# Post-norm decoder layer on one core: value projection cut into four parts, a second bank for three projections, max rows sent ahead of stacks

## What is computed

```python
x = layernorm(x + attn(x))          # 16 heads of 32, causal, q k v o projections with bias
x = layernorm(x + wkv(x, ctx))      # keys = x, values = ctx, a recurrence over 256 tokens in log space
x = layernorm(x + ffn(x))           # gate = softmax(x @ W_gate.T), top 1 of 16 heads picks k and v of a token;
                                    # causal attention of 16 query heads against that one k, v
```

## Time and profile before

| | |
|---|---|
| median of 3 runs | 1622.03 us |
| the profiled execution | 1626.53 us, its span 1624.7 us |
| TensorE matmuls | 1423.6 us busy, 88% |
| VectorE | 1103.8 us, 68% |
| ScalarE | 644.2 us, 40% |
| GpSimd | 415.5 us, 26% |
| mean granted TensorE clock | 0.976 of full speed |

### The profile page before, as it was taken

One profiled execution on the slowest core, in us unless ns is written; L12 is line 12 of the kernel. 1 busy time (PEld: TensorE's weight loads), 2 busy tenths in 40 slices (PEclk: granted clock), 3 DMA queues, 4 the chain that ended last, 5 costly groups with the idle time before them and its releaser, 6 DMA issues.

```text
span 1624.7 us, 28990 instructions
## 1 busy us (share of the span) xinstructions
PE 1423.6 (88%) x9792; PEld 1129.7 (70%) x9792; DVE 1103.8 (68%) x2260; ACT 644.2 (40%) x1459; POOL 415.5 (26%) x550
## 2 busy tenths in 40 slices
PE   6879988898998989889899998989989898999866
PEld 5667777766777767777677777777777767777554
DVE  4375766858577676776758667685766858577665
ACT  3442533434344243533435344253433425353322
POOL 1251321414122140321314122141312414122130
PEclk9889999999999999999999999999999999999979
DMA  5432231333213232231333312233221333323111
GB/s 173 140 85 66 58 78 45 84 86 77 73 44 84 68 87 79 58 79 52 78 85 76 78 48 74 70 86 86 67 73 46 74 86 76 89 55 81 37 33 34
DMA packets 63214, 119.70 MB, mean 74 GB/s; under 512 B 14304, under 2 KB 32736, under 8 KB 63072
## 3 DMA queue, kind: packets, MB, share of 16 engines
q1 hardware_dynamic: 60400, 112.56, 27.6%
q10 hardware_dynamic: 2672, 5.24, 0.9%
HBM read 32.81 MB, written 8.39 MB: 25 GB/s over the span
## 4 chain that ended last, share of the span: by engine, by line
PE 54%; DVE 21%; ACT 7%; issue 7%; SPq 6%; DMA 4%; POOL 1%; DVEq 0%; ACTq 0%; POOLq 0%
PE pp L482 9%; PE pp L484 8%; PE pp L483 8%; PE po L580 5%; SPq L320 5%; DVE neg_max L1349 5%; DVE w_key L1426 4%; DMA q_stack<-max_rows 3%; PE po L584 2%; PE sq L528 2%; PE sq L522 2%; PE sk L507 2%; PE sq L507 2%; PE po L594 2%; PE sk L558 2%
## 5 line engine op out<-in xcount | busy, mean ns | idle before, releaser
L1010 ACT ACTIVATE prob<-sk 128x512 f32<-128x512 f32 x384 | 215.0, 594 | 433.2 <-PE sk L507 432.6
L1349 DVE TENSOR_REDUCE neg_max<-sq 128x2 f32<-128x512 f32 (+1 forms) x384 | 249.5, 676 | 54.1 <-PE sq L507 29.5
L482 PE MATMUL pp<-xt_hi,w_hi 128*128 128x256 f32 x728 | 220.6, 303 | 9.7 <-DVE w_lo L1336 7.1
L483 PE MATMUL pp<-xt_lo,w_hi 128*128 128x256 f32 x728 | 207.7, 285 | 0.0
L484 PE MATMUL pp<-xt_hi,w_lo 128*128 128x256 f32 x728 | 207.7, 285 | 0.0
L482 PE MATMUL pp<-w_hi,xt_hi 128*128 128x512 f32 x372 | 159.6, 429 | 27.5 <-DVE q_lo L1464 15.8
L482 PEld LDWEIGHTS pp<-xt_hi,w_hi 128*128 128x128 f32 x728 | 141.2, 194 | 17.4 <-issue 11.9
L483 PE MATMUL pp<-w_lo,xt_hi 128*128 128x512 f32 x372 | 148.5, 399 | 0.0
L484 PE MATMUL pp<-w_hi,xt_lo 128*128 128x512 f32 x372 | 148.4, 399 | 0.0
L1021 ACT ACTIVATE o_ch<-po 128x512 f32<-128x512 f32 x128 | 76.2, 595 | 181.8 <-PE po L584 181.8
L483 PEld LDWEIGHTS pp<-xt_lo,w_hi 128*128 128x128 f32 x728 | 141.4, 194 | 0.7
(11 more groups left out here) (216 smaller groups left out, 3372.2 us busy)
## 6 DMA issues: line engine op xcount, KB each, us to landing
q_stack<-q_hi SPq DMA_DIRECT2D x256, 128.0 KB, 2.3
q_stack<-q_lo SPq DMA_DIRECT2D x128, 128.0 KB, 2.4
k_stack<-k_hi SPq DMA_DIRECT2D x128, 128.0 KB, 2.3
x_raw<-in_xT SPq DMA_DIRECT2D x16, 512.0 KB, 3.5
k_stack<-k_lo SPq DMA_DIRECT2D x64, 128.0 KB, 2.3
w_val<-in_ctxT SPq DMA_DIRECT2D x62, 128.0 KB, 2.1
w_raw<-in_weights ACTq DMA_DIRECT2D x4, 1024.0 KB, 5.9
q_stack<-max_rows SPq DMA_DIRECT2D x256, 4.0 KB
```

The costliest lines, as they stand in the source:

```text
L482: T.matmul(out, lh, rh, start=(c == 0), stop=False, skip_group_check=True)
L483: T.matmul(out, lh, rl, start=False, stop=False, skip_group_check=True)
L1010: A.activation(dst, sk[n % 2][:], ACT.Exp, scale=SCALE).then_inc(s_exp, 1)
L1349: V.tensor_reduce(dst, src, AX.X, ALU.max, negate=True).then_inc(s_max, 1)
```

## The change

TensorE's list gets a new order in ten places; the second key and the second value projection of the gated sub-layer and the second output projection go to the bank `pw`; VectorE's list is reordered at the seam, around `gating` and around the picks; ScalarE swaps `copy_a(2)` and `row_hi_a(3)`; SyncE sends three instead of nine q stacks ahead of the max row of group 3 and the load of x. No arithmetic is added or taken away. `products` now takes a dictionary of hooks, one for each chunk.

```diff
 def bank_f(b, job):
-return po if is_last(b) and job in (PF_Q + 1, PF_K + 1, PF_V + 1) else pp
+if is_last(b):
+    return po if job in (PF_Q + 1, PF_K + 1, PF_V + 1) else pp
+return pw if job in (PF_K + 1, PF_V + 1) else pp
 def bank_of(b, job):
...
     max_a(t, 2)
...
         store(t - 2, x_t)
-    q_stacks(b, PF_JOBS, PF_Q, pf_free, range(NG - 1), a_sk, TILES * t, f_stk)
+    q_stacks(b, PF_JOBS, PF_Q, pf_free, range(1), a_sk, TILES * t, f_stk)
     max_a(t, 3)
     load_x(t, x_t)
-    q_stacks(b, None, None, None, range(NG - 1, NG), a_sk, TILES * t, f_stk)
+    q_stacks(b, None, None, None, range(1, NG), a_sk, TILES * t, f_stk)
     if not last:
...
     max_f(b, 0)
...
     for c in range(CC):
...
             each(c)
-        if middle is not None and c == at:
+        if isinstance(middle, dict):
+            if c in middle:
+                middle[c]()
+        elif middle is not None and c == at:
             middle()
...
         T.matmul(out, lh, rh, start=(c == 0), stop=False, skip_group_check=True)
...
         if isinstance(b, int) and b == 1 and PA_Q < job <= PA_V:
             pe.wait_ge(pa_free, PA_JOBS * b + job - 1)
-        elif job != PA_WO:
+        elif job < PA_WO:
             wait(pe, pa_free, PA_JOBS * b + job)
...
     elif job < PA_V:
-        mm = channels_out(bank_of(b, job), W_K, job - PA_K, each=each)
+        mm = channels_out(bank_of(b, job), W_K, job - PA_K, middle, each=each)
     elif job < PA_WO:
-        at = 1 if job == PA_V else CC // 2
-        mm = tokens_out(bank_of(b, job), W_V, job - PA_V, middle=middle, at=at, each=each)
+        mm = tokens_out(bank_of(b, job), W_V, job - PA_V, middle=middle, each=each)
     else:
-        mm = tokens_out(pp, W_O, job - PA_WO, k_hi, k_lo, each=each)
+        mm = tokens_out((pp, pw)[job - PA_WO], W_O, job - PA_WO, k_hi, k_lo, middle=middle, each=each)
     mm.then_inc(pa_job, 1)
 def project_f(b, job, middle=None):
...
     bank = bank_f(b, job)
...
         pe.wait_ge(f_norm, NG * b)
-    pe.wait_ge(pf_free, PF_JOBS * b + (job - 1 if is_last(b) and job > PF_Q else job))
+    if bank is pw and job == PF_K + 1:
+        pe.wait_ge(w_free, W_JOBS * (b + 1))
+    else:
+        two = job > PF_Q if is_last(b) else job >= PF_V
+        pe.wait_ge(pf_free, PF_JOBS * b + (job - 1 if two else job))
     if job < PF_K:
...
     elif job < PF_V:
-        mm = tokens_out(bank, W_FK, job - PF_K)
+        mm = tokens_out(bank, W_FK, job - PF_K, middle=middle)
     else:
-        mm = tokens_out(bank, W_FV, job - PF_V)
+        mm = tokens_out(bank, W_FV, job - PF_V, middle=middle, at=1)
     mm.then_inc(pf_job, 1)
 def key_transpose(b, s_before, before):
...
         sk_a(t, 0, 0, 1)
         sq_a(t, 1, 2)
-    project_a(t, PA_V + 1, scores)
+    project_a(t, PA_V + 1, {1: lambda: y_transpose(b, 0), 2: scores})
     sk_a(t, 0, 2)
...
     y_transpose(b, 1)
...
     wait(pe, a_norm, NG * t)
...
     sq_a(t, 2, 0, 1)
+    sk_a(t, 1, 0, 1)
     turn_a(t, 0)
-    sk_a(t, 1, 0, 1)
     sk_a(t, 1, 2)
...
     out_transpose(t, 0)
...
     gate_transpose(b)
...
     sq_a(t, 3, 2)
-    project_f(b, PF_K)
-    max_a(t, 3)
     values_a(t, 2)
+    project_f(b, PF_K, lambda: max_a(t, 3))
+    turn_a(t, 2)
     project_f(b, PF_K + 1)
-    turn_a(t, 2)
     sk_a(t, 3, 0, 1)
     out_transpose(t, 2)
...
     pe.wait_ge(f_free, F_JOBS * b + F_KT + 1)
     wait(pe, a_max, TILES * a_done)
-    sq_f(b, 0, 0, 1, 2)
+    sq_f(b, 0, 0, 1)
     values_a(t, 3)
-    max_f(b, 0)
-    project_f(b, PF_V + 1)
+    sq_f(b, 0, 2)
+    project_f(b, PF_V + 1, lambda: max_f(b, 0))
     turn_a(t, 3)
+    sq_f(b, 1, 0, 1)
     wait(pe, a_exp, TILES * a_done)
     sk_f(b, 0, 0, 1)
-    sq_f(b, 1, 0, 1)
-    sk_f(b, 0, 2)
     wait(pe, f_free, F_JOBS * b + F_M[0] + 1)
     out_transpose(t, 3)
+    sk_f(b, 0, 2)
     sq_f(b, 1, 2)
     wait(pe, a_norm, NG * a_done)
...
     max_f(b, 1, a_free, A_JOBS * a_done)
...
     turn_f(b, 0)
-    sk_f(b, 1, 0, 1)
-    project_a(t, PA_WO + 1)
+    project_a(t, PA_WO + 1, lambda: sk_f(b, 1, 0, 1))
     sq_f(b, 2, 0, 1)
     sk_f(b, 1, 2)
...
     sk_f(b, 2, 0, 1)
     sq_f(b, 3, 0, 1)
-    sk_f(b, 2, 2)
-    project_a(t + 1, PA_K)
+    project_a(t + 1, PA_K, lambda: sk_f(b, 2, 2))
     sq_f(b, 3, 2)
...
     values_f(b, 2)
...
     turn_f(b, 2)
     sk_f(b, 3, 0, 1)
-    sk_f(b, 3, 2)
-    values_f(b, 3)
-    wait(pe, f_max, TILES * t)
-    wait(pe, a_max, TILES * (t + 1))
-    sq_a(t + 1, 0, 0, 1, 2)
-    turn_f(b, 3)
-    def between():
-        y_transpose(t, 0)
-        max_a(t + 1, 0, f_free, F_JOBS * t)
-    project_a(t + 1, PA_V, between)
+    def values_and_scores():
+        values_f(b, 3)
+        wait(pe, f_max, TILES * t)
+        wait(pe, a_max, TILES * (t + 1))
+        sq_a(t + 1, 0, 0, 1)
+    def turn_and_scores():
+        turn_f(b, 3)
+        sq_a(t + 1, 0, 2)
+    project_a(t + 1, PA_V, {1: lambda: sk_f(b, 3, 2), 2: values_and_scores, 3: turn_and_scores})
+    max_a(t + 1, 0, f_free, F_JOBS * t)
     sq_a(t + 1, 1, 0, 1)
 def value_a(c, h):
...
     sq_a(1, 0, 0, 1, 2)
...
     sq_a(1, 1, 0, 1)
-    y_transpose(0, 0)
 def ending():
     b = LAST - 1
...
     out_hi(t, 1)
...
     gate_sums(b)
+    copy_a(t, 2)
     row_hi_a(t, 3)
-    copy_a(t, 2)
     exps_a(t, 3, 0, 1)
     out_hi(t, 2)
...
     if c == 0:
...
     dve.wait_ge(pa_job, PA_JOBS * b + PA_WO + c + 1)
-    V.tensor_tensor(x[:, c, :], pp[:], x[:, c, :], ALU.add).then_inc(pa_free, 1)
+    V.tensor_tensor(x[:, c, :], (pp, pw)[c][:], x[:, c, :], ALU.add).then_inc(pa_free, 1)
 def first_stats(ch, b, x):
     dve.wait_ge(pa_free, PA_JOBS * (b + 1))
...
     cols = slice(P * g, P * (g + 1))
     ch.link(V.tensor_tensor(x[:, :, cols], x[:, :, cols], o_tok[:], ALU.add))
+def last_third_residual(b, x):
+    ch = Chain(dve, dve_f, F_LINKS, b)
+    ch.n = F_LINKS - 3
+    third_residual(ch, b, NG - 1, x)
 def third_stats(b, x):
...
     ch.n = F_LINKS - 1
...
     cha = Chain(dve, dve_a, A_LINKS, t)
     chf, chy = Chain(dve, dve_f, F_LINKS, b), Chain(dve, dve_w, W_LINKS, b)
+    second_residual(b, 0, x_b)
     maxima_a(t, 1, 2)
+    if not (isinstance(t, int) and t < 2):
+        last_third_residual(t - 2, x_t)
     rows_a(t, 1)
...
     second_stats(chy, b, x_b)
...
     maxima_a(t, 3, 0, 1)
...
     fq_lo(b, 1)
+    maxima_a(t, 3, 2)
     gating(chf, b)
-    maxima_a(t, 3, 2)
     rows_a(t, 3)
...
     normalise_a(cha, t, 2)
...
     assert chf.n == F_LINK_K3
...
     gate_value(chf, b)
+    rows_f(b, 0)
     pick_value(chf, b, 0)
-    rows_f(b, 0)
     normalise_a(cha, t, 3)
...
     assert chf.n == F_LINK_PICKED + 1
...
     maxima_f(b, 3, 0, 1)
...
     sums(t, 1)
+    maxima_f(b, 3, 2)
     qk_lo(t + 1, PA_K)
-    maxima_f(b, 3, 2)
     rows_f(b, 3)
...
     recurrence_start(t, 2)
...
     rows_a(t + 1, 0)
...
     maxima_a(t + 1, 1, 0, 1)
-    second_residual(t, 0, x_t)
     divide(t, 3)
-    third_residual(chf, b, 3, x_b)
 V.memset(v_a[:, :, :, HD:HD + 1], 1.0)
...
     sums(0, 3)
...
     maxima_a(1, 1, 0, 1)
-    second_residual(0, 0, x_even)
     divide(0, 3)
 def ending(chf):
```

## The result

The changed kernel takes 1611.8 us (median) against 1622.03 before, 10 us or 0.6% less. The ratio of the two is given as 0.9915, 95% interval 0.9891 to 0.9939, which is 10 to 18 us. One of its five executions took 4234.3 us, where the other four took 1610.78 to 1612.43, and is left out of the ratio as disturbed. So the kernel is faster by 10 to 18 us where 34 were forecast (1588, range 1574 to 1608). The direction was right; the size was not.

A forecast was written before the change was run, and what follows sets the result against it. TensorE, busy 88% of the span, sets the time where it has work, so only its idle time can be won, with no single engine behind its waits. Terms summed to 33.9 us: 1588 against the median, range 1574 to 1608.

The forecast's parts named there:

- The seam: Around max_a(0) and max_a(1): the third residual leaves VectorE's list ahead of the maximum; gain 1.2 us in 14 rounds, 16.8.
- Behind max_a(1): sk_a(1) tiles 0 and 1 ahead of turn_a(0) make x2 late; loss 0.8 us in 15 rounds, 12.0.
- The second query and the key projection: Ahead of the first key projection, values_a(2) fills the 1.05 us wait for q_lo; 15 rounds, gain 15.8 us.
- The max row of group 3: At sk_a(3): sent behind three stacks, the row lands before TensorE needs it; 0.75 us in 15 rounds, gain 11.2.
- the clause on the load of x: SyncE's queue: six stacks and x's load move 2 us later or earlier, harmless as readers come over 10 us behind.
- Its own second case: Bound of 0 for the key stretch: VectorE's chain of pick, key transpose and kf_stack is as late.
- The gated scores' start: At sq_f(1) and sq_f(0): values_a(3) fills one wait, the other stays; gain 0.25 us in 15 rounds, 3.7.
- the key of t+1: Around projection K: 0.9 and 0.29 us hidden but mostly not kept; gain 0.1 in 14 rounds, 1.4 us.
- The cuts: Borders between split projection blocks: three cost 0.1 us each, 0.3 a round; loss 4.5 us, bound 9.
- The loop's edge: VectorE's 3.24 us pause ahead of the maximum stays; the same 1.1 to 1.2 us is gone in front of it.
- The rival called "nothing": VectorE's list as a whole paces the rounds, or a pause at the loop's edge grows; 1622 us, chance 0.06.
- the first rival: At x2_transpose: x2 is not late, or the seam gives more, so the 12 us loss goes; 1576 us, chance 0.17.

The follow-up runs named there:

- e12: The kernel of e1 with VectorE's seam alone changed (third residual of group 3 behind the maximum, second_residual(0) behind divide(3)); 1588.7 us, ratio 0.9791.
- e8: The kernel before with SyncE's part alone: three q stacks ahead of group 3's max row and the load of x, nine behind; 1623.3 us, ratio 0.9991.
- e9: The changed kernel with the load of x moved behind the stacks of groups 1 and 2, max row still early; 1596.6 us, ratio 0.9860.
- e1: The kernel before with the hardware loop of rounds 2 to 13 written out as straight code on all five engines; 1603.6 us, ratio 0.9879.
- e2: The changed kernel with the loop written out as straight code on all engines; 1578.1 us, ratio 0.9738.
- e11: The kernel of e6 with the load of x behind the stacks; 1554.8 us, ratio 0.9585.
- e6: The kernel of e2 with turn_a(0) put back ahead of sk_a(1) tiles 0 and 1; 1571.3 us, ratio 0.9655.
- e7: The changed kernel with straight code on TensorE alone, the other four engines keeping their loop; 1586.8 us, ratio 0.9763.
- e3: The changed kernel with the first y transpose back ahead of the loop's edge, directly ahead of max_a(0); 1594.2 us, ratio 0.9829.
- e10: The kernel of e5 with turn_a(0) first and the load of x behind the stacks, loop kept; 1558.3 us, ratio 0.9626.
- e5: The kernel of e3 with max_a(0) and the first y transpose moved ahead of V's last chunk; 1586.8 us, ratio 0.9755.

## Why the prediction was wrong

The steps, one by one:

- **The seam**, 16.8 us. Right in kind and size: VectorE was the bound there, and e12 brought 15 us, for 13 net expected. One wait was overlooked: V's first chunk comes straight behind turn_f(2) and sk_f(3), ahead of where `pp` is free, and now waits 0.69 for qk_lo of the second key half (L1461) in every round. It falls in the stretch that waits for VectorE anyway.
- **Behind max_a(1)**, -12.0. Right: 1.1 us were forecast at x2_transpose, 0.96 stand there, and undoing the swap gave 13 and 7 us.
- **The second query and the key projection**, 15.8. The wait of 1.05 is gone in all rounds. By itself it was not tried.
- **The max row of group 3**, 11.2. This is the term that failed first. Its mechanism holds (the row lands in time), its worth alone was 0 (e8). The step that failed is the clause on the load of x, "2 us later or earlier", with add_bo "over 10 us behind": in the trace of before the addition already came 3.3 us behind the load's issue and was waiting for it. The change sends the load 3.4 us earlier, and the addition lands on VectorE's picks. Its own second case, VectorE's chain as late as the max row, came true through a cause it didn't name. Cost in the changed kernel: 15 us (e9; 9 by the ratios). For e8 the collision is seen in the trace, but e8 with the load left in place was not run, so it is not shown that the 11 us would have come in without it.
- **The gated scores' start**, 3.7, and **the key of t+1**, 1.4. Nearly as forecast: the wait at sq_f(1) is 0.97 a round where 0.42 and 0.72 stood at two places, a little less gain than thought; the K stretch waits 0.36 and 0.41 for `pp` (L1461) where it had waited 0.93 and 0.28, a little more.
- **The cuts**, -4.5. Not measured apart.
- **The loop's edge.** This is the term that failed most: "it stays" was said of VectorE's pause, and TensorE's own of 2.08 us was not in the sum, since a later wait covered it. The change took that cover away and put y_transpose with a second pause of about 2 us right behind the jump. At the edge shown TensorE was idle for 4.7 of 6.4 us, and its clock was at half from the first pause until 8 us after it. The edges' cost went from 18 to 34 us (e1, e2; by the ratios from 20 to 29). The rival called "nothing" named a growing pause at the edge, with a chance of 0.06, but had no price for it and no place for the clock.

In the numbers: 1588 forecast, 15 for the collision and 16 for the dearer edges make 1619, 9 and 9 by the ratios make 1606; 1611.8 was measured, 1608 by the ratio. So these two account for the miss as far as the runs can tell, and the rest of the sum was right to some 7 us. An estimate of the change in straight code without the collision (e2 less what e11 won over e6) is 42 us under e1 by the medians and 34 by the ratios; the sum had 33.9. That agreement is one of totals: five of its eight terms were not tried by themselves. The range was stated a little wider than its own reasons: 27 / 2 and 4.5 us above 1588 are 1606, not 1608, and the first rival is 1576, not 1574.

## What to carry to other kernels

When a change removes the wait that came last at some point, price what that wait was hiding, above all at a loop's edge: there each engine has its own pause, only the longest shows, and TensorE's may bring the slow clock with it. When a load is moved, follow it to the instruction that it releases and ask which engine that one shares ports with at its new time; a row whose longest duration is six times its median, as here 1296 to 196 ns, can be the mark of such a meeting. Straight code for one engine or for all is a cheap test that tells a better order from a worse edge.

## What was not expected of the hardware

- A GpSimd addition of 2.54 us for two tiles made a cast of 64 columns take 1.06 us (up to 1.30) instead of 0.20, and a subtraction of 32 columns 1.20 instead of 0.19.
- TensorE's granted clock fell to its lower level (1.2 of 2.4 GHz; matmuls 0.43 us apart for 0.23) at each of the five edges of the changed kernel, where it had waited 1.08 for a maximum, worked for 1.4 us and paused 2.9 to 4.3 us. With straight code on TensorE alone (e7) it is 1.00 from 190 to 1400 us. The length of the first pause does not tell whether the clock falls: in e3 it fell at each edge behind 2.7 to 4.3 us, in e10 not at all behind 1.88 and somewhat behind 1.76.
- The pause on "issue" behind TensorE's jump varies by the turn, 1.8 to 4.3 us over e3, e5 and e10, with nothing in the profile that tells the turns apart.
- The straight code, 26328 instructions in the page of e11 against 28994 in that of e10, was in total never slower than the loop: e11 against e10 and e1 against the kernel before.
